# Wide attention: two pairs' value products in every second tick, another order of banks, row maxima head by head; narrow attention: norm pieces in even ticks and the first norm's statistics a tick later

## The reference, cut to what matters

```
for every layer:
    h = layernorm(x) * (1 + ca) + sa ;  x = x + ga * attention(h)
    h = layernorm(x) * (1 + cb) + sb ;  x = x + gb * ffn(h)

layer 0 attention: q, k, v = split(h @ wqkv.T), 16 heads of 64
    q, k = rope(rmsnorm(q)), rope(rmsnorm(k))
    attn = softmax(where(causal, q @ k.T * 64**-0.5, -inf));  out = (attn @ v) @ wo.T
layer 1 attention: attn = softmax(q @ k.T * 64**-0.5 + bias[relative bucket]), no mask
layer 1 ffn: x = ln1(h + attention(h)), 16 heads of 8, no mask;  then ln2(x + moe(x))
layer 2 attention: rope, causal, 16 heads of 8
```

## Time and profile before

| | us |
|---|---|
| median of three runs | 3001.3 |
| profiled execution, its own time | 2998.88 |
| span of its records | 2996.8 |

### The profile page before, as it was taken

The page is one execution under the profiler, slowest core; times in us unless marked ns, Lnnn a source line. Parts: engine busy times, 40 slices in busy tenths (PEclk is TensorE's granted clock), DMA queues, the critical chain, the costliest instruction groups (busy, mean ns, idle before and its releaser), DMA issues.

```text
span 2996.8 us, 68983 instructions
## 1 busy us (share of the span) xinstructions
PE 2778.0 (93%) x25484; PEld 1870.1 (62%) x25484; DVE 2119.2 (71%) x5800; ACT 1705.1 (57%) x4109; POOL 1044.3 (35%) x1420
## 2 busy tenths in 40 slices
PE   6999999989999999999999798999989988999897
PEld 2666666666666666666666455567756665666675
DVE  6888888865666556666666688855667776887674
ACT  3877777773333367777776466644325544343665
POOL 6877877841000001111111345412243331104441
PEclk9999999999999999999999899999989999999999
DMA  3101111123000011111110555300035443245760
GB/s 104 30 16 29 30 30 30 30 72 100 1 15 1 1 35 30 30 30 30 30 30 20 152 142 132 92 1 15 1 103 132 128 114 87 58 100 131 200 172 26
DMA packets 194060, 188.01 MB, mean 63 GB/s; under 512 B 14544, under 2 KB 170256, under 8 KB 192960
## 3 DMA queue, kind: packets, MB, share of 16 engines
q1 hardware_dynamic: 193728, 183.61, 24.0%
HBM read 130.24 MB, written 53.31 MB: 61 GB/s over the span
## 4 chain that ended last, share of the span: by engine, by line
PE 65%; DVE 16%; ACT 6%; issue 5%; SPq 4%; DMA 2%; POOL 2%; DVEq 0%; ACTq 0%; POOLq 0%
PE pb L160 59%; ACT big L932 4%; SPq L1854 4%; PE pb L629 3%; DVE big L2173 2%; DVE big L802 2%; ACT big L157 2%; DVE big L785 1%; DVE big L231 1%; DVE big L713 1%; DMA big<-parts 1%; PE pb L562 1%; DVE big L784 1%; PE pb L2144 1%; DVE big L176 1%
## 5 line engine op out<-in xcount | busy, mean ns | idle before, releaser
L160 PE MATMUL pb<-big 64*128 64x256 bf16 (+13 forms) x20300 | 2512.9, 330 | 138.0 <-DVE big L2173 55.8
L160 PEld LDWEIGHTS pb<-big 128*128 128x128 f32 (+5 forms) x20300 | 1571.7, 145 | 877.6 <-issue 534.0
L157 ACT ACTIVATE big<-pb 128x512 f32<-128x512 f32 (+7 forms) x1444 | 825.1, 619 | 568.2 <-PE pb L160 324.8
L157 ACT ACTIVATE big<-pb,big 128x512 f32<-128x512 f32 (+2 forms) x536 | 315.3, 615 | 575.4 <-PE pb L160 482.3
L2173 DVE TENSOR_REDUCE big<-pb 128x4 f32<-128x1024 f32 (+1 forms) x256 | 278.2, 1087 | 111.6 <-PE pb L160 108.3
L171 POOL TENSOR_TENSOR big<-big 128x128 f32<-128x128 f32 x192 | 84.8, 456 | 682.0 <-DVE big L168 682.0
L932 ACT ACTIVATE big<-big 128x256 f32<-128x256 f32 x512 | 253.8, 497 | 70.5 <-DVE big L807 68.5
L932 ACT ACTIVATE big<-pb,big 128x128 f32<-128x128 f32 (+1 forms) x512 | 255.2, 512 | 67.5 <-DVE big L787 67.5
L1011 POOL TENSOR_TENSOR big<-big 128x512 f32<-128x512 f32 x128 | 159.7, 1275 | 247.6 <-DMA big<-recip 247.6
L802 DVE CUSTOM_DVE_ANT_0 big<-pb,big 128x256 f32<-128x256 f32 x512 | 186.6, 421 | 79.4 <-PE pb L160 79.2
L1528 DVE SCALAR_TENSOR_TENSOR big<-pb,big 128x128 f32<-128x128 f32 x512 | 144.1, 344 | 139.2 <-PE pb L160 138.4
(11 more groups left out here) (145 smaller groups left out, 2257.9 us busy)
## 6 DMA issues: line engine op xcount, KB each, us to landing
big<-parts SPq DMA_DIRECT2D x96, 512.0 KB, 4.1
parts<-big SPq DMA_DIRECT2D x384, 96.0 KB, 2.3
big<-recip SPq DMA_DIRECT2D x64, 512.0 KB, 6.7
big<-comb SPq DMA_DIRECT2D x32, 512.0 KB, 8.1
parts<-big SPq DMA_DIRECT2D x192, 64.0 KB, 2.1
big<-gates SPq DMA_DIRECT2D x8, 1024.0 KB, 6.4
big<-in_wf SPq DMA_DIRECT2D x1, 3072.0 KB, 14.8
big<-scratch SPq DMA_DIRECT2D x1, 3072.0 KB, 17.4
```

The costliest lines, as they stand in the source:

```text
L157: return e.activation(o, i, f, bias=bias, scale=scale)
L160: return e.matmul(o, l, r_, start=start, stop=stop, skip_group_check=True)
```

## The change

1. `take_tick` and the lists of TensorE and VectorE: projection and transposes now stand ahead of the transpose of the reciprocal sums (and, on VectorE, the projection's part ahead of its copy). v's last quarter moves from u = 7 to u = 5. The wide norms' statistics and normalizing are done one block earlier, and the norm's transposes at u = 0 of the block in which they stood at u = 7.
2. `value(t - 3)` and `value(t - 2)` stand together in odd ticks, none in even ones. `TS` has a third buffer, in the place of `WM` (and of the end of `WF`); VectorE waits for the last product at the end of the stage, and layer 2's modulation weights are loaded later, in the narrow stage.
3. Layer 1's row maxima: negation and release after each head, so two small negations a tick, and the exponentials in the order of heads.
4. Narrow stages: norm pieces at u = 2 and 4 instead of 3 and 5; layer 1's `ln1` statistics and their power in a step "z", a tick behind "c".

A second negation stands in the middle, behind the first head's two adds. The diff, cut to its core:

```diff
-            TS = [alloc(2 * width) for _ in range(2)]
+            TS = [alloc(2 * width) for _ in range(2)] + [WM if causal else big[:, spare_at:spare_at + 1024]]
-            v_at = (2, 3, 4, 7)
+            v_at = (2, 3, 4, 5)
-            def norm_at(a, u):
-
-                return u == 7 and a % 2 == 1 and a < 15
+            def normed_in(a):
+
+                if a == -1 or causal and a == 1:
+                    return (a + 1) // 2
+                return a // 2 + 1 if 2 * (ahead - 1) <= a < 14 and a % 2 == 0 else None
+
+            def turned_in(a, u):
+
+                if a == -1 or causal and a == 1:
+                    return (a + 1) // 2 if u == 7 else None
+                return (a + 1) // 2 if a < 15 and a % 2 == 1 and u == 0 else None
...
-                    tensor_sums(e, t)
                     tensor_project(e, a, u)
                     tensor_turn(e, b, u)
+                    tensor_sums(e, t)
                     tensor_extra(e, t, a, b, u)
                     if t < 128:
                         scores(e, t)
                     if 0 <= t - 1 < 128:
                         turn(e, t - 1)
-                    if 0 <= t - 2 < 128:
+                    if t >= 3 and t % 2:
+                        value(e, t - 3)
                         value(e, t - 2)
...
-                t.then_inc(own_v.sem, own_v.up())
-                e.wait_ge(own_v.sem, own_v.n)
-                e.tensor_scalar(nm, nm, -1.0, None, ALU.mult).then_inc(pair_maxed, 1)
+                    t.then_inc(own_v.sem, own_v.up())
+                    e.wait_ge(own_v.sem, own_v.n)
+                    e.tensor_scalar(nm[:, 2 * i:2 * i + 2], nm[:, 2 * i:2 * i + 2], -1.0, None, ALU.mult).then_inc(pair_maxed, 1)
 
             def ts_writable(e, p):
-                if p >= 2:
-                    e.wait_ge(pair_valued, p0 + p - 1)
+                if p >= 3:
+                    e.wait_ge(pair_valued, p0 + p - 2)
...
-                    vector_spread(e, t)
                     vector_project(e, a, u)
+                    vector_spread(e, t)
...
+                e.wait_ge(pair_valued, p0 + 128)
...
+                for n in range(4):
+                    qt, i = (n // 2, n % 2) if causal else (n % 2, n // 2)
+                    if n == 2 and not causal:
+                        e.wait_ge(pair_maxed, p0 + 2 * p + 2)
...
-                    found += [(c, piece) for at, piece in (((3, "normed0"), (5, "normed1"), (7, "turn")) if b % 2 else
-                                                           ((3, "stats0"), (5, "stats1"))) if at == i]
+                    found += [(c, piece) for at, piece in (((2, "normed0"), (4, "normed1"), (7, "turn")) if b % 2 else
+                                                           ((2, "stats0"), (4, "stats1"))) if at == i]
...
-                return [(step, (t - late) // 8) for step, late in (("back0", 17), ("back1", 17), ("a", 19), ("c", 21), ("d", 24))
+                return [(step, (t - late) // 8) for step, late in (("back0", 17), ("back1", 17), ("a", 19), ("c", 21), ("z", 22), ("d", 24))
...
-                    if not causal:
-                        e.wait_ge(s.free, s.n)
-                        for qt in range(2):
-                            n = 2 * b + qt
-                            stats_vector(e, own, [Z[qt]], 4 + n % 4, z_mean)
+                elif step == "z" and not causal:
+                    s = slots["c", b]
+                    e.wait_ge(s.free, s.n)
+                    for qt in range(2):
+                        n = 2 * b + qt
+                        stats_vector(e, own, [Z[qt]], 4 + n % 4, z_mean)
```

More of the change, by code:

```diff
@@ L489, in take_tick @@
                     take("turn", b, u, ring=ring)
+                for step, c in posts(t):
+                    if step == "turn":
+                        take(step, c, ring=ring)
                 if 0 <= b < 16 and u in v_at:
@@ L494, in take_tick @@
                         take(step, c, ring=ring)
-                if norm_at(a, u):
-                    take("ln", (a + 1) // 2, ring=ring)
+                if turned_in(a, u) is not None:
+                    take("ln", turned_in(a, u), ring=ring)
             norm = Norm(own_v, own_g, MODS[layer % 2], 0, slots, r0)
@@ L584, in tensor_extra @@
                         x.then_inc(s.full, 1)
-                if norm_at(a, u):
-                    norm.turn(e, (a + 1) // 2)
+                if turned_in(a, u) is not None:
+                    norm.turn(e, turned_in(a, u))
             def tensor_v(e, b, n):
@@ L760, in vector_extra @@
                     vector_v(e, b, v_at.index(u))
[L761 removed]
+                c = normed_in(a)
+                if c is not None:
                     if u == 0:
[L763 removed]
+                        norm.stats(e, c)
                     elif u in (3, 4):
[L765 removed]
+                        norm.normed(e, c, 2 * u - 6, 2 * u - 4)
             def vector_v(e, b, n):
@@ L920, in exps @@
                 s, b, j = p % 2, p // 8, p % 8
-                e.wait_ge(pair_maxed, p0 + p + 1)
+                e.wait_ge(pair_maxed, p0 + (p + 1 if causal else 2 * p + 1))
                 if p >= 2:
@@ L925, in exps @@
                     e.wait_ge(recip_made, b0 + b - 1)
-                for qt in range(2):
+                for n in range(4):
+                    qt, i = (n // 2, n % 2) if causal else (n % 2, n // 2)
                     at = 0 if qt == 0 else width - 256
                     w = 128 if causal and qt == 0 else 256
[L929 to L934, removed]
+                    if n == 2 and not causal:
+                        e.wait_ge(pair_maxed, p0 + 2 * p + 2)
+                    ps, h = PS[s][:, i, at:at + w], 2 * j + i
+                    t = e.activation(ps, banks[2 * s + i][:, at:at + w] if causal else ps, ACT.Exp, bias=NM[s][:, n:n + 1],
+                                     scale=rstd_q(b)[:, qt, h:h + 1] if causal else 1.0,
+                                     accum_out=SM[b % 2][:, 2 * h + qt:2 * h + qt + 1])
                 t.then_inc(pair_exped, 1)
@@ L1001, in gpsimd_tick @@
                         gpsimd_rstd(e, a, 0)
-                if u == 1 and norm_at(a, 7):
-                    norm.rstd(e, (a + 1) // 2)
+                if u == 1 and normed_in(a) is not None:
+                    norm.rstd(e, normed_in(a))
                 for step, c in posts(t):
@@ L2375, in gpsimd_post @@
                         residual_gpsimd(e, r0 + n, n)
-                    elif step == "c":
+                    elif step == "z" and not causal:
                         e.wait_ge(z_mean, n + 1)
@@ L2425, in own_tail @@
             def own_tail(i):
-                return (("back0", 15), ("back1", 15)) if i == 0 else ((("a", "c", "d")[i - 1], 15),)
+                return ((("back0", 15), ("back1", 15)), (("a", 15),), (("c", 15), ("z", 15)), (("d", 15),))[i]
             def tail_do(post):
@@ L2436, in narrow_attention @@
                           tensor_hosted, vector_hosted, scalar_hosted, gpsimd_hosted, sync_hosted)
-            own_end = Guest(4, lambda i: [take(step, b, ring=BK[6:8]) for step, b in own_tail(i) if step != "d"],
+            own_end = Guest(4, lambda i: [take(step, b, ring=BK[6:8]) for step, b in own_tail(i) if step not in "zd"],
                             tail_do(tensor_post), tail_do(vector_post), tail_do(scalar_post), tail_do(gpsimd_post), nothing)
```

25 lines of the change are left out of this document (11 added, 14 removed).

## The result

The changed kernel takes 2946.85 us (median of 4 runs, 2944.14 to 2949.75), the kernel before, in runs of the same session, 2999.94 us (2997.64 to 3003.85). The ratio is 0.9822, 95% interval 0.9805 to 0.9839: 53 us less. The forecast was 2945 us. The profiled execution took 2949.75 us with a span of 2947.7.

What follows compares the result with a forecast made beforehand. TensorE was taken as the bound, busy 91 to 98%, with its waits and own columns to gain; -27 - 5 - 16 - 10 + 2 = -56 us from 2998.9 gives 2943, as a median 2945 us, range 2925 to 2962.

Steps and rivals of the forecast that it cites:

- Layer 0's waits (3.0 us of stalls in 39.7): Layer 0's wide stage: 3.0 us of a 39.7 us block are stalls; the waits for reciprocal and c1's bank go.
- no wait of the sums' transpose for the reciprocal: Sign of being right: TensorE's wait there, 0.82 us a block in layer 0, is gone behind projection and transposes.
- Pairing, 0.16 us for two ticks: Layer 0's wide stage: two value products together save TensorE 0.16 us in two ticks, 0.64 us a block.
- Even ticks shorter than the chain: Layer 0: scores, maxima, exponentials, transposes outlast even ticks' work, 1.9 us of stalls, 37.9 us a block, 27 us gained.
- Layer 1: the number by luck: Layer 1's wide stage: -0.3 to -0.6 us a block, even ticks at least 3.6 us, 5 us gained in all.
- The chain of rows 5: Layer 1's wide stage before: scores' end to last exponential's end, given as 4.0 us, expected 3.5 head by head.
- Rival D: GpSimd's lock catches both negations, one in a short tick: +0.8 us in 16 blocks, 2958 us; chance 0.10.
- Narrow stage of layer 1: One VectorE piece a tick shortens the block from 16.3 to 15.0 us: 16 us gained.
- Narrow stage of layer 2: Double ticks and the DMA wait for q's and k's parts ease: block 16.5 us for 17.5, 10 us gained.
- The sum: Whole kernel: -27 - 5 - 16 - 10 + 2 = -56 us, forecast 2945 us.
- the 2 us for the ends of the wide stages: Last two blocks of each wide stage: ticks at the chain, odd ones grow, +1 us each stage.
- Rival E: Wide stages: even ticks can't shrink while odd ones grow by 0.64 and 0.87 us: +50, 3051 us; chance 0.05.

Runs made afterwards that it cites:

- e2: Wide stages' order alone (projection ahead of the sums' transpose, v's last quarter at u = 5, norm a block earlier) on the kernel before: 2971.17 us, ratio 0.9903.
- e5: The changed kernel with one value product in each tick again, third TS buffer kept: 2934.87 us, ratio 0.9789 to the kernel before.
- e3: Layer 1's row maxima released head by head alone, put into the kernel before: 2997.63 us, ratio 0.9986.
- e9: The changed kernel with single value products, late statistics and layer 1's copy of probabilities between the two heads' maxima: 2948.17 us, ratio 0.9820 to the kernel before.
- e1: Pairing of value products alone, with third TS buffer and later modulation loads, put into the kernel before: 3053.53 us, ratio 1.017.

## Why the prediction was right

**Layer 0's waits (3.0 us of stalls in 39.7).** Right. e2 shows the part alone. One sign failed: "no wait of the sums' transpose for the reciprocal". In layer 0 it is 4.2 us in 496, 0.76 us in every block with statistics: the reciprocal stands behind the row maxima, and these behind the statistics. In layer 1 it rose from 0.2 to 8.8 us.

**Pairing, 0.16 us for two ticks.** Right where no wait binds: 10.77 for 10.93 us.

**Even ticks shorter than the chain.** Right, and the step on which most hung: forecast 4.5 and 3.6 us at u = 0 (measured 4.63 and 3.68), 3.9 at u = 2 (3.85), 4.3 at u = 4 (4.3 and 4.5), the block 37.9 (37.8 by the window), 27 us (26). At u = 4 it is the chain in six of the 13 blocks; in five it is the wait for the bank, which the prediction doesn't have. I worked the sum only for the whole change, though, and so did not see that the forecast had a better kernel in it: with single products the same chain costs less, 10 us in e5.

**Layer 1: the number by luck.** The forecast was -5 us, measured were -8; a tick of 3.6 us came out at 3.70 and a block of 37.4 at 37.5. That the copy would be last behind a second negation was right for u = 2 and 4. But the prediction made its gain out of pairing (-0.6 us a block, +0.3 for stalls) and gave nothing to the order, and it is the other way round: from its first to its last tick the stage is 7 us shorter with the order alone (e2), 4 with the maxima alone (e3) and 17 with both (e5), and pairing takes 9 of them back, since idle time grew by 1.06 us a block with it and not by 0.3. Of the 8 us, 3 are in the 13 steady blocks; the rest is in the first ticks and the last two blocks, where +1 had been forecast. (The chain of rows 5, from 1305.00 to 1308.90, is 3.9 us, not 4.0.)

**Rival D, GpSimd's lock on both negations.** It did hold both up in 12 of the 13 blocks (the first took 0.22 to 1.13 us, the second 0.52 or 0.53, for 0.17), but in tick 3, and odd ticks are 5.36 us long and hide it. In 11 of 13 blocks tick 4 is 3.70 to 3.74 us. Where TensorE's work in tick 3 is 4.5 us and the negations stand apart, as in e9, the tick is 0.7 us longer, near D's 0.8.

**Narrow stage of layer 1: the term that was mis-sized.** The forecast was 16 us and a block of 15.0 us, measured were 12 and 15.2. The blocks are 15.0 and 15.4 us in turns: in every second one a tick is 2.37 us instead of 1.85, 2.6 of the 4 us. VectorE and GpSimd there:

```profile
1741.06 1.31 DVE L232 TENSOR_SCALAR big<-big 128x128 f32<-128x128 f32 x2
1742.29 1.21 DVE L2185 TENSOR_REDUCE big<-pb 128x4 f32<-128x1024 f32 x1
```

```profile
1740.53 1.09 POOL L1848 TENSOR_TENSOR big<-big 128x512 f32<-128x512 f32 x1
1741.68 0.61 POOL L1850 CAST big<-big 128x512 bf16<-128x512 f32 x1
```

I gave normalizing 0.65 us. Moved to u = 4 it meets the splitting of q and k on GpSimd (lines 1848 and 1850) and takes 1.31. That GpSimd can hold up a small operation of VectorE was read from L807 and not carried over to this stage.

**Narrow stage of layer 2.** The forecast was 10 us and a block of 16.5 us, measured were 10.5 and 16.6. No wait for the DMA of the parts is left in the wait table of these eleven blocks.

**The sum.** The four stages are 56 us shorter, as forecast. That is luck in part: layer 1's narrow stage gave 4 us less than its term, layer 1's wide stage 3 us more, and the 2 us for the ends of the wide stages didn't come.

**Rival E, slower.** Its mechanism, even ticks that can't shrink while odd ones grow, gives +91 us for pairing alone; its +50 has 41 us of gains from other parts in it. e1 measured +51, so some of the even ticks did shrink (u = 2 of layer 0 from 4.51 to 3.85 us); that 50 and 51 are so near is chance. For the whole change E was wrong, since the order took away c1's wait and most of the one for the reciprocal in layer 0, both of which stood in even ticks.

## What to carry to other kernels

When each tick has work of one engine and a chain through others, a tick costs the larger of the two, so evening out the ticks can beat bundling work. Here a bundle gained 0.16 us over two ticks that had no wait, and lost up to 0.87 us where the tick that gave up its work ended with a wait already. Work out each part of a change alone by the same steps as the whole, for a part can cost time inside a change that gains. A wait that is last by a tenth of a microsecond is worth a tenth: look what ends right behind it, and what the moved work will meet, before moving work for it.

## What the runs showed of the hardware

- An operation of VectorE with all operands in SBUF can stand for most of a GpSimd instruction: a negation of 128x4 values took 0.17 us and, beside L1011 (1.24 us each), 1.30 us; a `tensor_tensor` of 128x4 took 0.16 us and, beside the same scaling in layer 0, 0.87 and 1.04; two normalizings took 0.60 us (1242.69 in the changed kernel) and, beside the splitting, 1.31. Row maxima from PSUM kept their 1.2 us beside the splitting (1742.29).
- Two value products together took 0.16 us less of TensorE's time than the same two in ticks of their own (10.77 for 10.93 us in layer 0; 10.69 for 10.84 at the same place in layer 1). That it is the change between operations of other shapes is the prediction's reading; no run isolates it.
- The unchanged stages behind the last narrow one took 483.2 to 488.9 us over twelve profiled executions of twelve kernels; a difference below 6 us between two single executions is no finding by itself.
